# A transformer block with expert routing on one core: the last feed-forward layers rebuilt, and the opening's transfers put in another order

## The chip, the cores and the metric

The kernel runs on one core of a Trainium2 chip (trn2). The metric is the device time of one execution in microseconds (us). The five engines are TensorE (PE), VectorE (DVE), ScalarE (ACT), GpSimd (POOL) and SyncE (SP), which only issues transfers here. Each engine works through its own list of instructions in order, and engines wait for each other by semaphores. PSUM has eight banks of 128 partitions x 512 float32.

## The reference, cut to what matters

There are 8 batches of 256 tokens, width D = 256, 16 heads of 16.

```python
x = x + xattn0(layernorm(x), ctx, mask, W, b)      # "A" segments: masked softmax attention, then @ W.T + b
x = x + ffn0(layernorm(x), weight)                 # Hadamard, 4-bit quantised input, ternary weight
# third layer ("C" segments): attention with a bias per head, then a feed-forward layer
q, k, v = split(x_q @ Wq.T), split(x_kv @ Wk.T), split(x_kv @ Wv.T)
o = softmax(q @ k.T / 4 + bias) @ v
y = x_q + o @ Wo.T
h = gelu(layer_norm(y, g1, be1) @ W1.T + b1, approximate=False)     # 256 -> 1024
y = y + h @ W2.T + b2                                               # 1024 -> 256
x = x + layer_norm(y, g2, be2)
# fourth layer: each of 8 experts takes its 512 best tokens of all 2048
scores = softmax(layernorm(x) @ Wr); G, idx = top_k(scores.T, 512)
X_e = gelu(layernorm(x)[idx] @ W1[e] + b1[e]) @ W2[e] + b2[e]
out = x + scatter_add(G * X_e)
```

The routing (`top_k` over all 2048 tokens) cannot start before the last batch has gone through all three layers.

## The kernel before, in words

**Attention.** 16 segments run one after the other: A0, A1, A2, C0, A3, C1, ..., A7, C5, C6, C7, each of 16 units (2 query tiles x 8 pairs of heads). A loop counts slots `t`. In slot t, PE computes the scores of unit t+2 and transposes the probabilities of unit t (`ps_t`), and multiplies unit t-2 with the values (`ps_o`). DVE adds mask or bias and finds the row's extreme (`neg`, `neg_max`), ACT takes the exponential (`probs`) and the high half of the transposed probabilities (`p_hi`), DVE the low half (`p_lo`). Four units make a half: ACT copies it (`o_raw`), POOL adds its parts and normalises it (`attn`). Slot `ALL_UNITS` = 256 is the first without a new unit.

**What lies between the units.** `slots_of(b)` gives for each batch the slots at which the steps of its other layers stand on each engine: a table, not a planner. In a slot the units come first. The steps named below: `oc` (transposes of `attn`), `wo` (attention's output weights), `y` (sum and norm F), `z` (transposes of the normed rows), `f1` (first feed-forward weights, 8 pieces of two matmuls, into `ps_m[0]` and `ps_m[1]` in turn, copied to `hidT` with the bias by ACT two pieces at a time), `gelu` (Gelu in place on `hidT`), `f2` (second weights, into `ps_m[1]`), `y_ffn`, `ln_g`, `g_scale`, `x3` (sum, norm G with its two row vectors on POOL, sum into `x_all`), `ln_r`, `xr`, `logit` (norm R, its transposes and the routing logits).

**Stacks.** Before a segment, the two halves of k and q (`part_h` by ACT, `part_l`) go to `parts_dram` and come back in another layout: `k_stack` by four transfers into 32 partitions each, `q_stack` by eight into 16 partitions each. `q_stack` is zeroed once before (one memset of 128x4096 for each of two buffers). The stack of segment A1 lies where the ternary weight `w_b` is prepared (DVE `ve_start` in slots 0 to 2), so its loads wait for `wb_copied`.

**The opening.** SP's list stands in the code in its order: first inputs, mask and values of A0, `w_b`, row vectors, then the slots -16 to -1 (parts out, stacks in), then the weights.

## Time and profile before

| | us |
|---|---|
| median of 3 runs (983.73 to 984.74) | 983.77 |
| the profiled execution, own time | 983.23 |
| its span | 981.4 |
| busy PE / DVE / ACT / POOL | 769.3 / 660.2 / 616.5 / 430.6 |
| first scores of segment A0 | 29.46 |
| last unit's values copied | 654.28 |
| logits of the last batch end on PE | 712.07 |

Profile times count from the start of the span; the execution takes 1.83 us more than the span. No engine is busy throughout (PE 78%), and the shares are means over four very different stages: an opening in which almost only transfers run, attention, a tail after the last unit with the rest of batches 5, 6 and 7, and routing with the experts. So each stage is read by itself.

### The profile page before, as it was taken

Reading aid. Unit: us, or ns where it says so; the run is one execution under the profiler, and the core shown is the slowest. Engines: PE = TensorE matmul, PEld = TensorE weight load, DVE = VectorE, ACT = ScalarE, POOL = GpSimd, SP = SyncE. Lnnn points to the kernel's source line nnn. Section 1 sums busy time; section 2 is a strip of 40 time slices with the busy share of each in tenths; the row PEclk is TensorE's granted clock in tenths of the full one; section 3 lists DMA queues with packets and bytes.
Section 4 is the critical chain, followed back from the end, with each engine's and each line's share of the span. In section 5 each row is a group of like instructions: output and inputs, shape, how many; then the busy total and the mean of one; then the engine's idle time right before and its main releaser. Section 6 shows DMA issues by size and latency. Waiting matters only on the chain. (4 is left out here: it accounts for less than half of the span.)

```text
span 981.4 us, 19294 instructions
## 1 busy us (share of the span) xinstructions
PE 769.3 (78%) x6377; PEld 676.4 (69%) x6377; DVE 660.2 (67%) x2037; ACT 616.5 (63%) x1275; POOL 430.6 (44%) x626
## 2 busy tenths in 40 slices
PE   0566887887897987987989878878532799999995
PEld 0556776776786776876878768766421588888885
DVE  2686799786885986886787677542176366666651
ACT  1485777787787778679669758762010566666662
POOL 5154245264453554355244244143202456666654
PEclk9798789898998998999899998899655799999998
DMA  8598458668278477566645849200040234455532
GB/s 210 150 263 239 96 109 208 194 134 201 92 158 193 109 161 202 132 142 182 140 118 137 181 136 236 77 22 22 21 129 19 91 107 121 126 130 130 129 65 33
DMA packets 100290, 131.14 MB, mean 134 GB/s; under 512 B 8160, under 2 KB 72160, under 8 KB 100192
## 3 DMA queue, kind: packets, MB, share of 16 engines
q1 hardware_dynamic: 94048, 121.52, 48.8%
q0 software_dynamic: 6144, 8.39, 4.9%
q8 instruction: 52, 0.85, 0.4%
q14 instruction: 46, 0.38, 0.1%
HBM read 104.72 MB, written 25.17 MB: 132 GB/s over the span
## 5 line engine op out<-in xcount | busy, mean ns | idle before, releaser
L810 ACT ACTIVATE probs<-neg,neg_max 128x256 f32<-128x256 f32 x512 | 233.1, 507 | 108.5 <-DVE neg_max L659 105.4
L666 DVE TENSOR_TENSOR p_lo<-ps_t,p_hi 128x512 f16<-128x512 f32 x256 | 176.4, 689 | 108.5 <-ACT p_hi L817 108.4
L393 PE MATMUL ps_t<-ident,probs 128*128 128x128 f32 x1024 | 171.9, 294 | 59.8 <-ACT probs L810 59.3
L383 PE MATMUL ps_s<-k_stack,q_stack 128*128 128x256 f32 x512 | 147.2, 371 | 40.3 <-DMA q_stack<-parts_dram 21.3
L393 PEld LDWEIGHTS ps_t<-ident,probs 128*128 128x128 f32 x1024 | 124.3, 149 | 76.9 <-ACT probs L810 76.6
L817 ACT ACTIVATE p_hi<-ps_t 128x512 f16<-128x512 f32 x256 | 150.5, 588 | 27.5 <-PE ps_t L393 26.2
L383 PEld LDWEIGHTS ps_s<-k_stack,q_stack 128*128 128x128 f32 x512 | 94.6, 205 | 56.6 <-issue 30.8
L659 DVE CUSTOM_DVE_ANT_0 neg<-ps_s,bias_t 128x256 f32<-128x256 f32 x256 | 96.7, 415 | 13.8 <-PE ps_s L383 11.1
L1023 POOL TENSOR_TENSOR o_sum<-o_raw 128x128 f32<-128x128 f32 x64 | 30.2, 472 | 165.4 <-ACT o_raw L896 165.4
L659 DVE CUSTOM_DVE_ANT_0 neg<-ps_s,mask_add 128x256 f32<-128x256 f32 x224 | 84.1, 414 | 22.5 <-PE ps_s L383 22.3
L1329 DVE TENSOR_TENSOR hid_l<-hid_e,hid_h 128x512 fp32r<-128x512 f32 x64 | 69.4, 1115 | 40.2 <-ACT hid_e L1433 21.0
L413 PE MATMUL ps_o<-v_parts,p_hi 128*128 128x49 bf16 x1024 | 90.9, 189 | 0.9 <-DVE p_lo L666 0.9
L413 PE MATMUL ps_o<-v_parts,p_lo 128*128 128x49 bf16 x1024 | 89.4, 187 | 0.0
L1469 POOL DMA_INDIRECT out<-y_g,idx x32 | 52.8, 1649 | 67.7 <-ACT y_g L1447 59.5
L572 PE MATMUL ps_m<-w,hidT 128*128 128x256 f32 x256 | 76.0, 437 | 6.1 <-DVE part_l L673 5.3
L413 PEld LDWEIGHTS ps_o<-v_parts,p_hi 128*128 128x128 f16 x1024 | 79.2, 100 | 1.5 <-issue 1.3
L1399 PE MATMUL ps_o<-w_h,hid_h 128*128 128x256 f32 x256 | 75.3, 294 | 2.8 <-DVE hid_l L1329 2.7
L1399 PE MATMUL ps_o<-w_l,hid_h 128*128 128x256 f32 x256 | 72.3, 283 | 0.0
L1399 PE MATMUL ps_o<-w_h,hid_l 128*128 128x256 f32 x256 | 72.3, 282 | 0.0
L413 PEld LDWEIGHTS ps_o<-v_parts,p_lo 128*128 128x128 f16 x1024 | 68.1, 100 | 4.3
L555 PE MATMUL ps_m<-nrmT,w 128*128 128x256 f32 x256 | 68.8, 397 | 1.1 <-ACT nrmT L869 1.1
L1455 POOL DMA_INDIRECT xg<-normed_dram,idx x32 | 36.3, 1133 | 62.3 <-DVE idx L1302 45.7
(231 smaller groups left out, 1750.9 us busy)
## 6 DMA issues: line engine op xcount, KB each, us to landing
bias_t<-in_bias SPq DMA_DIRECT2D x64, 512.0 KB, 6.7
k_stack<-parts_dram SPq DMA_DIRECT2D x64, 256.0 KB, 4.3
q_stack<-parts_dram SPq DMA_DIRECT2D x128, 128.0 KB, 4.8
parts_dram<-part_h SPq DMA_DIRECT2D x32, 256.0 KB, 3.4
parts_dram<-part_l SPq DMA_DIRECT2D x32, 256.0 KB, 2.6
w1e<-in_w1e SPq DMA_DIRECT2D x8, 1024.0 KB
w2e<-in_w2e SPq DMA_DIRECT2D x8, 1024.0 KB, 5.7
ctxT_A<-in_ctxT SPq DMA_DIRECT2D x8, 256.0 KB, 5.7
```

The costliest lines, as they stand in the source:

```text
L383: ins = nc.tensor.matmul(ps_s[U % 2][:, i * SEQ:(i + 1) * SEQ], q_stack[g % 2][:, h % 2, j, c, qt * P:(qt + 1) * P], k_stack[g % 2][:, j, ...
L393: ins = nc.tensor.matmul(ps_t[U % 2][:, (i * QT + kb) * P:(i * QT + kb + 1) * P], probs[:, U % 2, i, kb * P:(kb + 1) * P], ident[:, :], st ...
L413: ins = nc.tensor.matmul(ps_o[half][:, col:col + VW], part[:, U % 4, (i * QT + kb) * P:(i * QT + kb + 1) * P], v_parts[g % 2][:, kb, h, :] ...
L555: ins = nc.tensor.matmul(ps_m[hc // 2 % 2][:, (hc % 2) * SEQ:(hc % 2 + 1) * SEQ], w_1[:, c, hc * P:(hc + 1) * P], nrmT[:, c, :], start=(c ...
L572: ins = nc.tensor.matmul(ps_m[1][:, tile * D:(tile + 1) * D], hidT[:, hc, tile * P:(tile + 1) * P], w_2[:, hc, :], start=(hc == 0), stop=( ...
L659: ins = nc.vector.tensor_tensor_reduce(neg[:, U % 4, i, :], ps_s[U % 2][:, i * SEQ:(i + 1) * SEQ], add, -1.0, 3.0e38, ALU.add, ALU.min, ne ...
L666: nc.vector.tensor_tensor(p_lo[:, U % 4, :], ps_t[U % 2][:, :], p_hi[:, U % 4, :], ALU.subtract).then_inc(lo_ready, 1)
L810: ins = nc.scalar.activation(probs[:, U % 2, i, :], neg[:, U % 4, i, :], ACT.Exp, bias=neg_max[:, U % 4, i:i + 1], scale=-1.0)
L817: nc.scalar.activation(p_hi[:, U % 4, :], ps_t[U % 2][:, :], ACT.Copy).then_inc(hi_ready, 1)
L1329: nc.vector.tensor_tensor(hid_l[:, hc, :], hid_e[:, hc % 4, :], hid_h[:, hc, :].bitcast(F32), ALU.subtract).then_inc(S["hid_ready"], 1)
L1399: ins = nc.tensor.matmul(ps_o[i][:, (st % 2) * D:(st % 2 + 1) * D], hid[:, hc, st * P:(st + 1) * P], w[:, hc, :], start=(n == 0), stop=(n ...
L1469: nc.gpsimd.indirect_dma_start(out, bass.IndirectOffsetOnAxis(ap=idx[e % 4][:, st:st + 1], axis=0), y_g[:, st, :], None, compute_op=ALU.ad ...
```

## The change

Three things.

**The last feed-forward layers.** In batch 6, `f1` stands earlier, two pieces to a slot in the last five slots of attention. In batch 7, `f1` writes to four banks that attention no longer uses (`ps_s[0]`, `ps_s[1]`, `ps_t[0]`, `ps_t[1]`), ACT takes Gelu with the bias straight from them into `hidT`, and `f2` goes quarter by quarter into `ps_o[0]` and `ps_o[1]`, each quarter as soon as its Gelu is there. Norm G of batch 7 is two DVE instructions for each tile, with one sum on POOL ahead of it. The slots of batch 7 and of `xr` and `logit` of batches 5 and 6 are set anew. ACT loads the Gelu table by an instruction on a scratch tile at slot 256.

**The opening.** `parts_out` and the stack loads of A0 stand directly behind the four first loads, everything else behind them. The zeroing of `q_stack[0]` moves from DVE to POOL, and A0's `part_l` of k from POOL to DVE. POOL and DVE no longer wait for the constants. `x_biased` of batch 0 stands behind the mask and values in POOL's list, and so the zeroing of `q_stack[1]` too.

**One scratch instruction** has ACT load its first table ahead of its first wait.

```diff
-LAST_SLOT = ALL_UNITS + 3 * UNITS
+LAST_SLOT = ALL_UNITS + 2 * UNITS
@@ slots_of
+        at.update(ln_a=early, ln_a_apply=early + 1, x_biased=early + 15, mask=early + 3, va=early + 4)
...
+    if b == 7:
+        at.update(oc=end + 2, wo=(end + 4, end + 4), y=end + 4, ln_f_apply=end + 5, yb=end + 6, z=end + 7,
...
@@ TensorE, batch 7
+        ps_last = [ps_s[0], ps_s[1], ps_t[0], ps_t[1]]
+        def pe_last_ffn(pe, t):
...
+                    for hc in (2 * n, 2 * n + 1):
+                        for c in range(DC):
+                            ins = nc.tensor.matmul(ps_last[n][:, (hc % 2) * SEQ:(hc % 2 + 1) * SEQ],
+                                                   w_1[:, c, hc * P:(hc + 1) * P], nrmT[:, c, :],
+                                                   start=(c == 0), stop=(c == DC - 1))
+                    ins.then_inc(S["f1_out"], 1)
+            for n in range(FC // 2):
+                if t == AT[b]["f2"][n]:
+                    pe.wait_ge(S["gelu_done"], b + n + 1)
...
+                        for tile in range(QT):
+                            ins = nc.tensor.matmul(ps_o[tile][:, 0:D], hidT[:, hc, tile * P:(tile + 1) * P],
+                                                   w_2[:, hc, :], start=(hc == 0), stop=(hc == FC - 1))
@@ ScalarE
+            for n in range(FC // 2 if b == NB - 1 else 0):
+                if t == at["f1"][2 * n]:
+                    ac.wait_ge(S["f1_out"], b * 4 + n + 1)
...
+                        ins = nc.scalar.activation(hidT[:, hc, :], ps_last[n][:, i * SEQ:(i + 1) * SEQ], ACT.Gelu,
+                                                   bias=cols[:, 2 * DC + hc:2 * DC + hc + 1])
+                if t == ALL_UNITS:
+                    nc.scalar.activation(warm[:, 1:2], warm[:, 0:1], ACT.Gelu)
@@ VectorE
+            if t == at["k_a"] and b == 0:
+                ve.wait_ge(S["part_h"], 1)
+                nc.vector.tensor_tensor(part_l[:, :, :], ctxT[A][:, :, :], part_h[:, :, :].bitcast(F32),
+                                        ALU.subtract).then_inc(S["part_l"], 1)
...
+            if t == at["g_scale"] and b == NB - 1:
...
+                    ins = nc.vector.scalar_tensor_tensor(nrm["G"][:, n, :], y_of(b)[:, n, :], mv["G"][:, n, 0:1],
+                                                         rows[:, 2, :], ALU.subtract, ALU.mult)
...
+                    ins = nc.vector.scalar_tensor_tensor(x_all[:, 2 * b + n, :], nrm["G"][:, n, :], rstd["G"][:, n:n + 1],
+                                                         x_all[:, 2 * b + n, :], ALU.mult, ALU.add)
...
             if s == 0:
+                ve.wait_ge(ld["const"], 16 * N_CONST)
+                nc.vector.tensor_copy(ident_b[:, :], ident[:, :])
@@ GpSimd
+            if t == at["ln_g"] - 1 and b == NB - 1:
+                nc.gpsimd.tensor_tensor(xpair(b), xpair(b), rows[:, 3:4, :].to_broadcast([P, QT, D]),
+                                        ALU.add).then_inc(S["g_added"], 1)
...
         def po_start(po):
+            nc.gpsimd.memset(q_stack[0][:, :, :, :, :].bitcast(F32), 0.0).then_inc(S["q_zero_0"], 1)
@@ SyncE
+            parts_out(A, 0, "k")
+            k_in(A, 0, (0, 1))
+            parts_out(A, 0, "q")
+            k_in(A, 0, (2, 3))
+            q_in(A, 0)
             load_mask(0)
             load_va(0)
+            load_a(1)
+            sp.dma_start(x_all[:, QT:2 * QT, :], a["x"][1]).then_inc(ld["x1"], 16)
             sp.dma_start(w_b[:, :, :], a["w_b"]).then_inc(ld["w_b"], 16)
...
-            for t in range(-UNITS, 0):
-                slot(t)
```

SP's list in the opening, before (`parts_dram` holds the halves on their way to the stacks):

```order
L1618 DMA ident<-in_ident 128x128
L1497 DMA mask_int<-in_mask 128x2x256
L1501 DMA v_raw_A<-in_ctx 128x2x256
L1621 DMA w_b<-in_w_b 128x2x256
L1623 DMA rows<-in_rows 128x256 x4
L1624 DMA x_all<-in_x 128x2x256
L1526 DMA parts_dram<-part_h 128x512
L1528 DMA parts_dram<-part_l 128x512
L1543 DMA k_stack<-parts_dram 32x4x512 x4
L1493 DMA ctxT_A<-in_ctxT 128x2x256
```

And now:

```order
L1696 DMA ident<-in_ident 128x128
L1604 DMA parts_dram<-part_h 128x512
L1606 DMA parts_dram<-part_l 128x512
L1621 DMA k_stack<-parts_dram 32x4x512
L1621 DMA k_stack<-parts_dram 32x4x512
L1604 DMA parts_dram<-part_h 128x512
L1606 DMA parts_dram<-part_l 128x512
L1621 DMA k_stack<-parts_dram 32x4x512
L1621 DMA k_stack<-parts_dram 32x4x512
```

Nothing stands between the constants and the parts any more, and mask, values, `w_b` and rows come after the eight loads of `q_stack`.

POOL's list behind the first norm, before:

```order
L953 TENSOR_TENSOR part_l<-ctxT_A,part_h 128x512
L958 TENSOR_TENSOR x_all<-x_all,rows 128x512
L963 TENSOR_SCALAR mask_add<-mask_int 128x512
L934 CAST v_parts<-v_raw_A 128x16x16 x2
L936 TENSOR_TENSOR v_rest<-v_raw_A,v_parts 128x256 x2
L938 CAST v_parts<-v_rest 128x16x16 x2
L940 TENSOR_TENSOR v_raw_A<-v_rest,v_parts 128x256 x2
L942 CAST v_parts<-v_raw_A 128x16x16 x2
L1110 MEMSET q_stack 128x4096
L953 TENSOR_TENSOR part_l<-ctxT_A,part_h 128x512
```

And now:

```order
L1039 TENSOR_SCALAR mask_add<-mask_int 128x512
L1010 CAST v_parts<-v_raw_A 128x16x16 x2
L1012 TENSOR_TENSOR v_rest<-v_raw_A,v_parts 128x256 x2
L1014 CAST v_parts<-v_rest 128x16x16 x2
L1016 TENSOR_TENSOR v_raw_A<-v_rest,v_parts 128x256 x2
L1018 CAST v_parts<-v_raw_A 128x16x16 x2
L1034 TENSOR_TENSOR x_all<-x_all,rows 128x512
L1188 MEMSET q_stack 128x4096
L1029 TENSOR_TENSOR part_l<-ctxT_A,part_h 128x512
```

The chain starts with the mask, whose load is now late in SP's list; the sum of rows and the second memset follow the values.

PE's list after the last unit, before (`nrm_R` are the transposes for routing, `attn` and `w_o` attention's output, L555 is `f1`, L572 `f2`):

```order
L555 MATMUL ps_m<-nrmT,w 128x256 x6
L327 MATMUL ps_m<-ident,nrm_R 128x128 x4
L589 MATMUL ps_m<-w_r,nrmT_c 128x8 x4
L327 MATMUL ps_m<-ident,attn 128x128 x4
L335 MATMUL ps_m<-w_o,nrmT 128x256 x2
L572 MATMUL ps_m<-w,hidT 128x256 x4
L335 MATMUL ps_m<-w_o,nrmT 128x256 x2
L572 MATMUL ps_m<-w,hidT 128x256 x12
L327 MATMUL ps_m<-ident,nrm_F 128x128 x4
L555 MATMUL ps_m<-nrmT,w 128x256 x16
L327 MATMUL ps_m<-ident,nrm_R 128x128 x4
L589 MATMUL ps_m<-w_r,nrmT_c 128x8 x4
```

And now (L580 is `f2` of batch 6, L618 and L629 are `f1` and `f2` of batch 7):

```order
L335 MATMUL ps_m<-ident,attn 128x128 x4
L580 MATMUL ps_m<-w,hidT 128x256 x2
L343 MATMUL ps_m<-w_o,nrmT 128x256 x4
L580 MATMUL ps_m<-w,hidT 128x256 x10
L335 MATMUL ps_m<-ident,nrm_F 128x128 x4
L580 MATMUL ps_m<-w,hidT 128x256 x4
L618 MATMUL ps_s<-nrmT,w 128x256 x8
L618 MATMUL ps_t<-nrmT,w 128x256 x4
L629 MATMUL ps_o<-w,hidT 128x256 x4
L618 MATMUL ps_t<-nrmT,w 128x256 x4
L629 MATMUL ps_o<-w,hidT 128x256 x12
L335 MATMUL ps_m<-ident,nrm_R 128x128 x4
```

Three of `f1`'s pieces of batch 6 are gone from here, the transposes and logits of batch 6 stand behind `f2` of batch 7 instead of between its two layers, and `f1` and `f2` of batch 7 interleave.

## Rows read from the trace of the kernel before

**Rows 1.** Busy time by stage, the tail: stretch, length, each engine, PE clock, DMA
```profile
654.28:712.07 57.79, 37.54 (x160) 30.66 (x159) 11.38 (x36) 15.25 (x25) 14.83 (x20) 0.81 0.06 22
```
**Rows 2.** Timeline of SP's issues, opening: start, length, line, what
```profile
6.61 0.47 SPq L1526 DMA_DIRECT2D parts_dram<-part_h  x1
...
11.36 1.75 SPq L1543 DMA_DIRECT2D k_stack<-parts_dram  x4
...
19.84 3.60 SPq L1555 DMA_DIRECT2D q_stack<-parts_dram  x8
23.48 0.43 SPq L1497 DMA_DIRECT2D mask_int<-in_mask  x1
```
**Rows 3.** Tile parts_dram, 0 to 47 us: issue to landing
```profile
DMA to landing us min/median/max: 2.0/4.6/6.3
```
**Rows 4.** Tile k_stack, the same
```profile
DMA to landing us min/median/max: 3.0/4.3/5.9
```
**Rows 5.** Tile q_stack, the same
```profile
DMA to landing us min/median/max: 2.9/4.7/6.3
```
**Rows 6.** Tile mask_int, the same
```profile
DMA to landing us min/median/max: 3.9/5.2/6.6
```
**Rows 7.** Timeline of DVE, opening and first units; idle before it in brackets
```profile
8.20 1.68 DVE L633 TENSOR_SCALAR nrm_A<-x_all,mv_A,rstd_A 128x256 f32<-128x256 f32 x2 [1.26 <-POOL rstd_A L923]
...
30.38 0.42 DVE L659 CUSTOM_DVE_ANT_0 neg<-ps_s,mask_add 128x256 f32<-128x256 f32 x1 [17.53 <-PE ps_s L383]
...
34.55 0.68 DVE L1068 TENSOR_REDUCE w_b_abs<-w_b 128x2 f32<-128x512 f32 x1
35.26 0.61 DVE L1069 TENSOR_SCALAR w_b_scale<-w_b_abs 128x2 f32<-128x2 f32 x1
...
36.31 0.42 DVE L659 CUSTOM_DVE_ANT_0 neg<-ps_s,mask_add 128x256 f32<-128x256 f32 x1
```
**Rows 8.** Timeline of POOL, the same
```profile
8.15 1.25 POOL L953 TENSOR_TENSOR part_l<-ctxT_A,part_h 128x512 fp32r<-128x512 f32 x1
...
11.39 1.95 POOL L963 TENSOR_SCALAR mask_add<-mask_int 128x512 f32<-128x512 int32 x1
13.40 0.76 POOL L934 CAST v_parts<-v_raw_A 128x256 bf16<-128x256 f32 x2
...
18.49 3.51 POOL L1110 MEMSET q_stack<- 128x4096 f32 x1
...
34.57 1.27 POOL L953 TENSOR_TENSOR part_l<-ctxT_A,part_h 128x512 fp32r<-128x512 f32 x1 [12.57 <-ACT part_h L822]
```
**Rows 9.** Timeline of PE, last unit and tail
```profile
649.92 0.66 PE L393 MATMUL ps_t<-ident,probs 128*128 128x128 f32 x4 [0.58 <-ACT probs L810]
...
662.98 2.07 PE L335 MATMUL ps_m<-w_o,nrmT 128*128 128x256 f32 x4 [2.24 <-ACT nrmT L865]
...
668.05 5.34 PE L572 MATMUL ps_m<-w,hidT 128*128 128x256 f32 x24
...
674.94 7.17 PE L555 MATMUL ps_m<-nrmT,w 128*128 128x256 f32 x32 [1.11 <-ACT nrmT L869]
...
687.54 10.04 PE L572 MATMUL ps_m<-w,hidT 128*128 128x256 f32 x32 [0.84 <-ACT hidT L885]
708.40 1.12 PE L327 MATMUL ps_m<-ident,nrm_R 128*128 128x128 f32 x4 [10.82 <-DVE nrm_R L633]
```
**Rows 10.** Timeline of ACT, tail
```profile
659.16 1.28 ACT L885 ACT_TABLE_LOAD   x1
660.45 2.00 ACT L885 ACTIVATE hidT<-hidT 128x1024 f32<-128x1024 f32 x2
```
**Rows 11.** Timeline of DVE, tail
```profile
668.32 0.69 DVE L748 TENSOR_TENSOR y_attn<-ps_m,xq_res 128x512 f32<-128x512 f32 x1 [7.86 <-PE ps_m L335]
...
697.69 0.69 DVE L756 TENSOR_TENSOR y_attn<-ps_m,y_attn 128x512 f32<-128x512 f32 x1 [10.78 <-PE ps_m L572]
...
705.38 0.75 DVE L618 BATCH_NORM_STATS2 st_R<-x_all 128x6 f32<-128x256 f32 x2 [4.05 <-POOL x_all L1014]
```

## What the change should do to the time, predicted before it ran

> **What bounds the kernel now.** The page says that no engine is busy throughout, so I read by stages and took two of them: those in which the change moves something. In the stretches view of the tail the reader is to see 57.8 us in which PE is busy 37.5 and DVE, ACT and POOL 11 to 15 [rows 1]: a chain in which one engine at a time works and the others wait. The timelines of the tail show its links: attention's output weights at 662.98, norm F at 668.32, `f1` of batch 7 at 674.94, `f2` at 687.54, norm G at 697.69, norm R at 705.38, its transposes at 708.40 [rows 9 to 11]. Everything behind 708.40 (logits, routing, experts) is unchanged and starts from it, so what the tail gives goes fully into the end.
>
> In the opening the chain is of transfers. SP's issues show the waits: `part_h` goes out at 6.61, but the first load of `k_stack`, which needs it, at 11.36; `q_stack`'s loads begin at 19.84 [rows 2] and the last lands at about 23.0 + 6.3 = 29.3 [rows 5]. DVE's first score pass is at 30.38 [rows 7]. Attention moves with that start: its loads for later segments hang on its own engines, so I carry a shift of the start to the end in full.
>
> **The opening, part by part.** Before, 1.5 MB of other loads lay ahead of `part_h` in SP's queue. Now only the first four do, and these have landed, since `part_h` waits for them. With the shortest landing, 2.0 [rows 3], the out-transfer issued at about 6.5 is there at 8.5, where it was 11.36. From there the queue is full and I add pieces. `k_stack`: first landing 11.4 + 3.0 = 14.4, last (issued 12.7) + 5.9 = 18.6 [rows 2, 4], so 1.4 us each. `q_stack`: 19.84 + 2.9 = 22.7 to 29.3 is 0.94 each [rows 2, 5]. Two further transfers of 256 KB lay between 18.6 and 19.84, so 0.6 each. New: first piece of k 11.5, second 12.9, the two parts of q 14.1 (they are ready: norm A at 8.20 no longer waits behind POOL's `part_l` [rows 7, 8]), two pieces of k 16.9, eight of q 24.5. The mask, before issued behind `q_stack` with a landing of 6.6, came at 23.48 + 6.6 = 30.1 [rows 2, 6], 0.75 behind the last q; now 25.25. That is a new wait: POOL needs 1.95 for it [rows 8], and the first pass cannot start before 27.3. Scores are ready earlier (25.7), so the mask is late next. Gain so far 30.38 - 27.4 = **3.0 us**. Its bounds: 1.5, if the landings after 8.5 keep the 3.0 of a queue's first piece at each wait, and 4.
>
> The price stands on DVE. Before, POOL had finished the values (13.40 to 18.49) and the zeroing of `q_stack[1]` (3.51) while DVE was idle [rows 8]. Now the values follow the mask (27.3 to 32.5), then the sum with rows (1.27, as the other additions of 128x512), then the memset (33.8 to 37.3), all beside DVE's burst for `w_b`, and DVE has little idle time there. The trace shows what POOL does to DVE's small instructions: `w_b_scale`, 128x2, took 0.61 and ended at 35.87, just as POOL's instruction of 34.57 + 1.27 did; and norm A's first pass from 8.20 to 9.88 spanned POOL's of 8.15 to 9.40 [rows 7, 8]. So some DVE instructions stand until POOL's is through. No row has a memset as POOL's part, so bounds: nothing (a memset does not block) and 3.5 (its whole length). By the nearest rows, in which the whole instruction was waited for, I take the whole. Working: DVE reaches the new cast of `ident_b` 4.2 behind its first pass (34.55 - 30.38), at 31.6; cast 0.5, reduction 0.7, `w_b_scale` behind the sum at 33.8, one `w_b_half`, then the memset has begun and the next waits until 37.3; POOL's own delay by DVE's cast adds about 0.3. The pass of unit 3, at 36.31 before [rows 7], comes at 37.9: **+1.6 us** net for the whole opening. Without the block by the memset it is at 34.3, -2.0.
>
> The Trainium skill, "SBUF — State Buffer", section "Who interferes with whom", says that DVE in its two-port modes and GpSimd take one shared port pair as a lock for the whole instruction. The two rows above agree; that a GpSimd memset holds it too, no row here shows. By that rule the opening costs as I forecast; by the memset's absence from the trace alone it could as well gain 2.0.
>
> Other edits of the opening are at nothing: the zeroing of `q_stack[0]` on POOL (3.5 us from about 1.7) is done at 5.2, ahead of the constants; the loads of `w_b` and rows land 3 to 6 us behind the mask, when DVE and POOL first want them, and if not, the wait falls on the same DVE stretch; ACT's first table load is hidden by the constants' load either way.
>
> **The tail, part by part.** (a) *End of attention to norm F of batch 7.* Before, the last probability transposes are at 649.92 [rows 9]. A pair of pieces of `f1` costs 8 records of 7.17/32 = 0.224, so 1.8 us; batch 6 has now four pairs in five slots instead of four single pieces. PE then transposes the last unit near 652.7 instead of 649.9, and `p_lo` of the last unit ends at 654.5. ACT: last bias copy to 654.7, table load 1.28 [rows 10], a copy for routing, then attention's copy at 656.8, where it was 654.28 [rows 1]. That is 2.5 late, and it is the table load that is late, in front of the copy. But then PE has nothing in its way: Gelu of batch 6 (2.00 [rows 10]) 657.3 to 659.3, `attn`'s transposes 659, their copy 660.1, one piece of `f2`, both halves of `wo` together. The first half of `wo` took 2.07 for 4 records, double of 0.224 each, after an idle time of 2.24 [rows 9]; I expect the same once. Norm F's sum starts at 664.3, before 668.32 [rows 11]: **-4.0**.
>
> (b) *To `f1` of batch 7.* Ten rows of `f2` (20 records x 5.34/24 = 4.45), transposes 0.6, eight more records 1.8 beside ACT's copy: 671.0. Before 674.94 - 668.32 = 6.6, now 6.7: **+0.1**.
>
> (c) *`f1` and `f2` of batch 7.* Before 674.94 to 697.69: 22.75, in it ACT's copies and Gelu (682 to 687.5) and `f2` in 10.04 where 32 records at the rate of `f2` of batch 6 take 7.1 [rows 9, 11]. Now PE never waits for all of Gelu: ACT's two instructions for a pair are below the pair's 1.8 on PE. 7.17 + 7.12 + 0.1 = 14.4: **-8.35**. Gelu from PSUM does not stand in the trace; bounds are 0.42 for one (the in-place 1.0 for 1024 columns scaled down, plus its start) and 1.0; only above 0.9 would ACT pace PE, at most +1.
>
> (d) *Norm G.* Before 697.69 to 705.38 = 7.7 [rows 11]. Now sum 0.85, statistics 1.1, the copy of batch 6's logits (PE does these behind `f2`: 2.6 us, so it is the logits that are late here, not POOL's root), two pairs of DVE instructions of 0.95: 4.6. **-3.1**. The 3.0 from 705.38 to 708.40 stay.
>
> Sum of the tail: -4.0 + 0.1 - 8.35 - 3.1 = -15.35. With the opening -15.35 + 1.6 = -13.8, from the profiled execution's 983.23 to 969.4. That execution lies 0.5 below the median of the runs shown, so the forecast is **970.0**.
>
> **Rivals.**
> *The memset does not block DVE.* For it: no row has one. Against: both rows in which POOL and a small DVE instruction meet. Then -15.35 - 2.0, so 966.4.
> *The tail gives less.* Attention's end loses more than it wins: pairs of `f1` delay scores, PE falls to 1.2 GHz more often in the short gaps between 656 and 660, and another 24 records run at double time. +5.4: about 975.4. For it: 2.07 in [rows 9]. Against: the granted clock of the tail was 0.81 with gaps of 5 to 11 us, which now shrink [rows 1].
> *Slower than before: PE stays at 1.2 GHz through the tail.* Its work from `wo` to the end of `f2` of batch 7 is 23.2 us at the full rate; all of it at double time is +23.2, so 970.0 + 23.2 = 993. The kernel becomes slower once more than 60% of that work (13.8 of 23.2) runs so. For it: `f2` at 687.54 ran at 0.31 per record, between both rates. Against: 674.94 to 682.1, after an idle time of 1.11, ran at 0.224 throughout, and the new tail has no longer gap before `f2` ends.
> *It does not do what it says in the opening.* If `q_stack`'s pieces wait for the parts of q longer than the queue is full, the first pass is no earlier than 29, and the opening costs 3.2: 971.6. I keep it inside the forecast's own range.
>
> **How the numbers follow.** Forecast 0.57, own range 967.5 to 973. No block by the memset 0.25, less in the tail 0.13, slow clock through the tail 0.03, something better than all of these 0.02. Range: down to 964, which takes in the second case with the bound of 4 us for the opening's gain, up to 975.5, which takes in most of the third. About 0.2% of the time, 2 us, is what a measurement can tell from no change. Faster 0.96, since only the slow clock in its worse half and an unforeseen wait reach 982; same 0.015; slower 0.025.
>
> **What would show it.** Opening: first load of `k_stack` at about 8.5; last of `q_stack` landed near 24.5; first pass at 27.4 with the idle time before it ended by POOL's mask; one DVE instruction of 128x2 or 128x256 with 2 to 3.5 us beside POOL's memset (right), or all below 0.7 (the second case); pass of unit 3 at 37.9. Tail, counted from the last probability transposes: attention's copy behind a table load; `f1` and `f2` of batch 7 together in 14 to 15 us with a granted clock near 1; from `y_ffn` to norm R 4.6 us. The forecast is wrong if `f2` shows waits for Gelu above 0.5 us each, if the stretch from the last unit's copy to norm R's transposes is over 44 us (before 54.1), or if the pass of unit 3 is outside 34 to 39.

## The result, and the profile after

The changed kernel takes 966.4 us (median of 4, 964.0 to 970.5) against 983.75 for the kernel before beside it: ratio 0.983, 95% interval 0.981 to 0.985. In a later comparison it took 963.1 (median of 6) against 984.7, ratio 0.979 (0.976 to 0.982). The forecast was 970.0 in 964.0 to 975.5.

The profiled execution is the longest of the first four: 970.47, span 968.6, against 983.23 and 981.4 before. Its 12.8 us split at two landmarks of the trace, each counted from the one before it. The first is ACT's copy of `o_raw` number 60 of 0 to 63 (half 60 below), which lies ahead of all that the change moves in the tail. The second is the first transpose of norm R's output of batch 7.

| stretch | before | after | difference | forecast |
|---|---|---|---|---|
| start to the pass of unit 3 | 36.31 | 36.95 | +0.64 | +1.6 |
| from there to the copy of half 60 | 585.26 | 589.23 | +3.97 | 0 |
| half 60 to norm R's transposes | 86.83 | 70.97 | -15.86 | -15.35 |
| from there to the end | 273.0 | 271.45 | -1.55 | 0 |

**The tail.** PE, after. A row is start, length, engine, line, operation, count, and in brackets the idle time before it and what ended it.

```profile
658.16 0.60 PE L401 MATMUL ps_t<-ident,probs 128*128 128x128 f32 x4
...
666.76 2.93 PE L343 MATMUL ps_m<-w_o,nrmT 128*128 128x256 f32 x8
669.53 4.48 PE L580 MATMUL ps_m<-w,hidT 128*128 128x256 f32 x20
...
676.01 3.62 PE L618 MATMUL ps_s<-nrmT,w 128*128 128x256 f32 x16
679.47 1.89 PE L618 MATMUL ps_t<-nrmT,w 128*128 128x256 f32 x8
681.19 1.89 PE L629 MATMUL ps_o<-w,hidT 128*128 128x256 f32 x8
682.92 1.89 PE L618 MATMUL ps_t<-nrmT,w 128*128 128x256 f32 x8
684.65 5.34 PE L629 MATMUL ps_o<-w,hidT 128*128 128x256 f32 x24
...
697.15 1.12 PE L335 MATMUL ps_m<-ident,nrm_R 128*128 128x128 f32 x4 [4.99 <-DVE nrm_R L674]
```

From 676.01 to 690 PE issues `f1` and `f2` of batch 7 with no gap; none of the five rows has a bracket. Before, the same 64 records stood with an idle stretch between them, and `f2` took 10.04 [rows 9]. The stretches of `f1` and `f2` in after: length, busy time of PE, PEld, DVE, ACT, POOL with counts, granted clock, DMA share, GB/s; then the whole tail, which answers to [rows 1]:

```profile
676.01:689.99 13.98, 13.98 (x67) 12.28 (x66) 4.69 (x13) 3.36 (x8) 6.89 (x8) 1.00 0.12 39
666.76:669.50 2.74, 2.74 (x9) 2.25 (x8) 0.00 (x0) 0.00 (x0) 0.00 (x0) 0.62 0.00 0
662.07:700.82 38.75, 32.21 (x144) 27.95 (x144) 12.85 (x39) 9.80 (x18) 12.24 (x18) 0.81 0.08 28
```

and in before the stretch in which `f2` of batch 7 ran:

```profile
687.54:697.60 10.06, 10.04 (x32) 8.04 (x32) 0.00 (x0) 0.00 (x0) 0.00 (x0) 0.71 0.00 0
```

The reader is to see the clock beside the length: 32 records of `f2` at a granted 0.71 take 10.04, and at 1.00 they take their 7.2 (1.89 + 5.34). The 8 records of `wo` ran at 0.62 and took 2.93; in another execution of the same code (`after_again` below) they took 1.95. ACT and DVE in the same tail, after:

```profile
660.20 1.28 ACT L975 ACT_TABLE_LOAD   x1
...
662.07 0.49 ACT L970 COPY o_raw<-ps_o 128x392 f32<-128x392 f32 x1
662.44 2.01 ACT L950 ACTIVATE hidT<-hidT 128x1024 f32<-128x1024 f32 x2
...
684.85 0.84 ACT L958 ACTIVATE hidT<-ps_t,cols 128x256 f32<-128x256 f32 x2 [2.61 <-PE ps_t L618]
```
```profile
669.80 0.69 DVE L793 TENSOR_TENSOR y_attn<-ps_m,xq_res 128x512 f32<-128x512 f32 x1 [5.49 <-PE ps_m L343]
...
690.10 0.75 DVE L806 TENSOR_TENSOR y_attn<-ps_o,y_attn 128x256 f32<-128x256 f32 x2 [2.27 <-PE ps_o L629]
...
692.29 0.89 DVE L817 SCALAR_TENSOR_TENSOR nrm_G<-y_attn,mv_G,rows 128x256 f32<-128x256 f32 x2
...
694.13 0.75 DVE L659 BATCH_NORM_STATS2 st_R<-x_all 128x6 f32<-128x256 f32 x2
```

A pair of Gelus from PSUM takes 0.84, under half of the pair's 1.8 on PE: ACT waits for PE here, not the reverse.

**The opening.** SP's issues, after:

```profile
5.98 0.33 SPq L1604 DMA_DIRECT2D parts_dram<-part_h  x1
...
8.03 0.80 SPq L1621 DMA_DIRECT2D k_stack<-parts_dram  x2
...
12.86 3.58 SPq L1633 DMA_DIRECT2D q_stack<-parts_dram  x8
16.49 0.43 SPq L1575 DMA_DIRECT2D mask_int<-in_mask  x1
```

`k_stack`'s first load goes out 3.3 us earlier than in [rows 2], `q_stack`'s 7.0 earlier. DVE and then POOL, after:

```profile
25.80 0.42 DVE L700 CUSTOM_DVE_ANT_0 neg<-ps_s,mask_add 128x256 f32<-128x256 f32 x1 [15.80 <-POOL mask_add L1039]
...
31.09 4.60 DVE L1147 TENSOR_SCALAR w_b_half<-w_b_scale 128x2 f32<-128x2 f32 x1
...
35.72 1.19 DVE L1148 TENSOR_SCALAR w_b_half<-w_b_scale 128x2 f32<-128x2 f32 x1
...
36.95 0.42 DVE L700 CUSTOM_DVE_ANT_0 neg<-ps_s,mask_add 128x256 f32<-128x256 f32 x1
```
```profile
23.81 1.95 POOL L1039 TENSOR_SCALAR mask_add<-mask_int 128x512 f32<-128x512 int32 x1 [17.86 <-DMA mask_int<-in_mask]
...
30.95 1.27 POOL L1034 TENSOR_TENSOR x_all<-x_all,rows 128x512 f32<-128x512 f32 x1
32.16 3.51 POOL L1188 MEMSET q_stack<- 128x4096 f32 x1
35.63 1.26 POOL L1029 TENSOR_TENSOR part_l<-ctxT_A,part_h 128x512 fp32r<-128x512 f32 x1
```

The first pass waits for the mask, as the bracket says, and begins 4.6 us earlier than in [rows 7]. Eleven us later all of that is gone: an instruction on 128x2 elements ends at 35.69, with POOL's memset at 35.67, and the next at 36.91, with POOL's subtraction at 36.89.

### The profile page after: what moved, and what is told of

It is laid out like the page before. It is cut to its first block and busy times, and to the rows that moved or that the text cites. A ratio compares the mean times of both kernels' runs of the same rounds, so it can differ in the third digit from the quotient of the medians.

```text
span 968.6 us, 19298 instructions
## 1 busy us (share of the span) xinstructions
PE 771.3 (80%) x6377; PEld 681.5 (70%) x6377; DVE 664.4 (69%) x2041; ACT 613.4 (63%) x1275; POOL 429.9 (44%) x624
## 5 line engine op out<-in xcount | busy, mean ns | idle before, releaser
L391 PE MATMUL ps_s<-k_stack,q_stack 128*128 128x256 f32 x512 | 150.0, 377 | 44.1 <-DVE neg_max L700 18.2
L700 DVE CUSTOM_DVE_ANT_0 neg<-ps_s,mask_add 128x256 f32<-128x256 f32 x224 | 83.9, 412 | 20.7 <-POOL mask_add L1039 15.8
L580 PE MATMUL ps_m<-w,hidT 128*128 128x256 f32 x224 | 68.1, 440 | 6.7 <-DVE part_l L714 6.7
L563 PE MATMUL ps_m<-nrmT,w 128*128 128x256 f32 x224 | 63.1, 408 | 0.2 <-ACT nrmT L934 0.2
```

What stands on the lines that cost most here:

```text
L391: ins = nc.tensor.matmul(ps_s[U % 2][:, i * SEQ:(i + 1) * SEQ], q_stack[g % 2][:, h % 2, j, c, qt * P:(qt + 1) * P], k_stack[g % 2][:, j, ...
L563: ins = nc.tensor.matmul(ps_m[hc // 2 % 2][:, (hc % 2) * SEQ:(hc % 2 + 1) * SEQ], w_1[:, c, hc * P:(hc + 1) * P], nrmT[:, c, :], start=(c ...
L580: ins = nc.tensor.matmul(ps_m[1][:, tile * D:(tile + 1) * D], hidT[:, hc, tile * P:(tile + 1) * P], w_2[:, hc, :], start=(hc == 0), stop=( ...
L700: ins = nc.vector.tensor_tensor_reduce(neg[:, U % 4, i, :], ps_s[U % 2][:, i * SEQ:(i + 1) * SEQ], add, -1.0, 3.0e38, ALU.add, ALU.min, ne ...
```

## The experiments

### The two halves apart, and the zeroing moved

`tail_only` is the kernel before with the changes of the tail alone, `open_only` with those of the opening alone:

```diff
 # tail_only
-LAST_SLOT = ALL_UNITS + 3 * UNITS
+LAST_SLOT = ALL_UNITS + 2 * UNITS
 ...
+        ps_last = [ps_s[0], ps_s[1], ps_t[0], ps_t[1]]
 # open_only
+            parts_out(A, 0, "k")
+            k_in(A, 0, (0, 1))
+            parts_out(A, 0, "q")
+            k_in(A, 0, (2, 3))
+            q_in(A, 0)
```

> The kernel before with only the rebuilt last feed-forward layers (slots of batches 5 to 7, four banks, Gelu from PSUM, f2 by quarters, norm G in two instructions, early Gelu table). Theory: the tail gives nearly everything and the opening nothing, because what its transfers gain is lost to POOL's block of DVE. Then this kernel is at 966 to 969 (ratio 0.982 to 0.985) and the stretch from the last unit's probability transposes to the transposes of norm R of batch 7 is 39 us (58.5 before). Rival: the opening contributed; then this kernel is at 970 or more.

> The kernel before with only the opening's new order. Theory: first score pass at 25.8 (30.4 before), but unit 3's pass at 37.0 (36.3 before), since one w_b_half of 128x2 stands 4.6 us beside POOL's sum and memset and the next 1.2 beside part_l; total 983.5 to 985, the same as before within noise. Rival: the opening helps although the trace of one execution does not show it, 979 to 981.

`early_zero` is the changed kernel with POOL's zeroing of `q_stack[1]` ahead of the mask's work:

```diff
-                if t == 0:
+                if t == -UNITS + 1:
                     po_zero_stack(po)
```

> The changed kernel with one edit: POOL zeroes q_stack[1] directly behind the first norm's root (about 6 us), when it has nothing to do, not at the first unit. Theory (POOL's memset holds DVE's two-port instructions for its whole length): w_b_half takes at most 1.3 beside the sum with rows, unit 3's pass comes at 32.5 to 33.5 instead of 37.0, and the kernel is 3.5 to 4.5 us faster than the changed one, 962 to 963. Rival (the 4.6 us of w_b_half have another cause, a late load or a semaphore): w_b_half stays at 4 or more and the time at 966.

`before_late_zero` does the opposite, in the kernel before: it holds the zeroing back until DVE is in its burst.

```diff
                 if t == 0:
+                    po.wait_ge(lo_ready, 1)
                     po_zero_stack(po)
```

> The kernel before with one edit: POOL's zeroing of q_stack[1] waits for the first low part (34.6) instead of running at 18.5. The loads stay as they are. Theory: w_b_scale at 35.3 stands until POOL's memset is over at 38.1, a following one until part_l is over at 39.4; unit 3's pass moves from 36.3 to 39.5 and the total by +3, to 987. Rival (DVE is not blocked by a memset): w_b_scale stays below 0.7 and the total at 984.

Measured, in one comparison (before: 983.94, median of 23; the trace's columns are from one execution each):

| kernel | time | ratio (95%) | first pass | pass of unit 3 | between |
|---|---|---|---|---|---|
| before | 983.94 | | 30.38 | 36.31 | 5.93 |
| `tail_only` | 963.11 | 0.980 (0.977 to 0.982) | 28.98 | 34.90 | 5.92 |
| `open_only` | 979.82 | 0.997 (0.995 to 0.999) | 22.49 | 33.64 | 11.15 |
| `early_zero` | 963.82 | 0.981 (0.978 to 0.984) | 28.26 | 35.96 | 7.70 |
| `before_late_zero` | 986.79 | 1.004 (1.001 to 1.006) | 30.55 | 39.86 | 9.31 |

The block is shown in both directions. POOL, then DVE, of `before_late_zero`:

```profile
34.86 3.51 POOL L1111 MEMSET q_stack<- 128x4096 f32 x1 [16.26 <-DVE p_lo L666]
38.34 1.26 POOL L953 TENSOR_TENSOR part_l<-ctxT_A,part_h 128x512 fp32r<-128x512 f32 x1
```
```profile
35.43 2.96 DVE L1070 TENSOR_SCALAR w_b_scale<-w_b_abs 128x2 f32<-128x2 f32 x1
...
38.43 1.19 DVE L1071 TENSOR_SCALAR w_b_half<-w_b_scale 128x2 f32<-128x2 f32 x1
...
39.86 0.42 DVE L659 CUSTOM_DVE_ANT_0 neg<-ps_s,mask_add 128x256 f32<-128x256 f32 x1
```

`w_b_scale` starts 0.57 behind the memset and ends at 38.39, 0.02 behind the memset's end. In [rows 7] the same instruction took 0.61. With the memset early, in `early_zero`, the 4.60 is gone from this place:

```profile
33.55 1.15 DVE L1147 TENSOR_SCALAR w_b_half<-w_b_scale 128x2 f32<-128x2 f32 x1
34.74 1.18 DVE L1148 TENSOR_SCALAR w_b_half<-w_b_scale 128x2 f32<-128x2 f32 x1
```

But the block has only moved. The early memset runs while DVE applies norm A, whose rows must leave as the parts of q. POOL and DVE of `early_zero`:

```profile
5.76 3.50 POOL L1188 MEMSET q_stack<- 128x4096 f32 x1
```
```profile
6.25 3.48 DVE L674 TENSOR_SCALAR nrm_A<-x_all,mv_A,rstd_A 128x256 f32<-128x256 f32 x2
```

and DVE of the changed kernel at the same place:

```profile
6.60 0.73 DVE L674 TENSOR_SCALAR nrm_A<-x_all,mv_A,rstd_A 128x256 f32<-128x256 f32 x2
```

SP issues the high part of q at 11.61 instead of 9.22, the first load of `q_stack` at 13.86 instead of 12.86 and the mask at 17.54 instead of 16.49, and the first pass comes at 28.26. In `open_early_zero` below it is the same (3.65, 11.58, 13.83, 17.50, first pass 28.51).

That a memset on POOL holds DVE is settled: late, it costs 3.4 us of trace (9.31 against 5.93; 11.15 against 7.70). The kernel before, which is the same in all but this wait, becomes 2.9 us longer by it (interval 1.4 to 5.7), as its theory said. `early_zero` met its theory in `w_b_half` (1.15, at most 1.3) and missed it in the pass of unit 3: 35.96 and not 32.5 to 33.5.

For the whole change the tail is the gain: alone it brings 20.8 us, more than its theory gave it, and its trace took 38.4 from the last probability transposes to norm R's (39 in the theory). The opening alone brings 4.1 (interval 1 to 5), which is its rival's time and not its theory's. The two don't add up: the whole change, at 0.983 and 0.979 in its two comparisons, is not faster than the tail alone at 0.980.

### The same kernel again, batch 6 at its old places, the opening with both, and the mask first

`after_again` has no edit. `old_slots_6` puts batch 6's `f1`, Gelu and `f2` and the logits of batches 5 and 6 back to where the kernel before has them, and batch 7 behind it:

```diff
     if b == 6:
-        at.update(f1=tuple(end - n for n in (5, 5, 4, 4, 3, 3, 2, 2)), f1_copy=(end - 4, end - 3, end - 2, end - 1),
-                  gelu=end + 1, f2=tuple(end + n for n in (3, 5, 5, 6, 6, 6, 8, 8)), y_ffn=end + 9, ln_g=end + 9,
 ...
+        at.update(gelu=end + 4, f2=tuple(end + n for n in (7, 7, 8, 8, 9, 9, 10, 10)), y_ffn=end + 10, ln_g=end + 10,
```

`open_early_zero` is `open_only` with the zeroing early. `mask_first` is `early_zero` with the mask and the values in SP's queue ahead of the last pieces of `k_stack`:

```diff
             parts_out(A, 0, "q")
-            k_in(A, 0, (2, 3))
-            q_in(A, 0)
             load_mask(0)
             load_va(0)
+            k_in(A, 0, (2, 3))
+            q_in(A, 0)
```

> The changed kernel once more, unchanged, to have its time and a second trace on the same chip as the next three. Theory: the time is 964 to 967; from the first score pass to unit 3's pass it is 11.15 us again, since POOL's instructions set it, while the first pass itself moves by a few us with the speed of the transfers (22.5 to 28.3 in three traces of this order so far); the second loss of attention (at the copies of 206 and 619 us) does not come back, since it was waits for bias loads and the clock of one execution. Rival: these losses belong to the change; then they stand at the same places.

> The changed kernel with batch 6's f1, Gelu and f2, and batch 7's attention output, at the slots of the kernel before; four banks, Gelu from PSUM, the quarters of f2 and the new norm G stay. Theory: this undoes the term from the end of attention to norm F (-3.1 to -4.9 in three traces), so from the copy of the half that ends near 620 us to norm F's sum of batch 7 it is 46 to 47 us instead of 42 to 43.6, and the total is 3 to 5 above the changed kernel. Rival: pairs of f1 in attention's last slots cost what they give later; then both are within 1 us.

> The kernel before with the opening's new order and POOL's zeroing of q_stack[1] at about 6 us instead of at the first unit; the tail is the old one. Theory: first pass as in the other kernels with this order, from it to unit 3's pass 7.7 us instead of 11.15, total 3.5 below the opening alone: 976 to 977. Rival (the opening alone gains by another way than its first pass): no difference to the opening alone, 979.8.

> The changed kernel with the early zeroing, the loads of A0's mask and values ahead of the second half of k_stack's loads instead of behind q_stack's, and the sum with rows of batch 0 at slot 4 instead of slot -1. Theory: POOL has done mask and values before the scores are there; the first pass follows the last load of q_stack by 1 to 1.3 us (2.5 in the changed kernel) though that load lands 1.3 later; from the first pass to unit 3's it is 6.2 to 7.3 us; 1 us below the kernel with the early zeroing alone, 4 to 5.5 below the changed one: 961 to 962. Rival: the two loads delay q_stack by more than they save, and it is no better than early zeroing alone.

Measured, in one comparison (before: 984.69, median of 17):

| kernel | time | ratio (95%) | pass of unit 3 | half 60 against before | half 60 to norm R's transposes |
|---|---|---|---|---|---|
| `after_again` | 963.14 | 0.979 (0.976 to 0.982) | 37.99 | -1.67 | 68.07 |
| `old_slots_6` | 969.81 | 0.985 (0.982 to 0.988) | 37.03 | +3.08 | 73.19 |
| `open_early_zero` | 981.12 | 0.996 (0.994 to 0.998) | 36.22 | -2.58 | 87.83 |
| `mask_first` | 961.28 | 0.978 (0.975 to 0.981) | 33.00 | -4.52 | 68.04 |

The same code reached half 60 at +4.61 in one execution and at -1.67 in the next. The +3.97 of the first table is so no cost of the change: from the pass of unit 3 to half 60 it took 589.2 in the first profile, 581.9 in this one and 585.3 before, and 581.0 to 587.6 in the other kernels. The -1.55 behind the tail is scatter too: that stretch, whose code nothing here changes, took 271.4 to 273.0 over all fourteen profiles. The largest step of the +3.97, 3.2 us, lies between halves 58 and 59, where DVE waited once for a transfer of the bias and the granted clock fell. From the view of waits (who for whom, us in total, times, longest) and that of stretches, after:

```profile
DVE neg L700 <- DMA bias_t<-in_bias: 3.0, 1, 3.0
```
```profile
607.40:618.90 11.50, 9.13 (x75) 8.15 (x73) 5.51 (x20) 7.41 (x19) 3.31 (x7) 0.85 0.96 263
```

and the same 75 records of PE in before, 3.2 us shorter:

```profile
606.00:614.30 8.30, 7.54 (x75) 6.85 (x73) 5.43 (x20) 7.35 (x19) 3.33 (x7) 1.00 1.07 334
```

`old_slots_6` shows that moving batch 6's `f1` into the last units of attention, with what follows it, is worth 0.6% (0.985 against 0.979; the intervals just clear each other), and the tail of its trace is 5.1 longer than that of `after_again`. Which of the moved steps brings how much, it doesn't tell. Its PE runs `wo` in two halves with pieces of batch 6's `f2` between them:

```profile
664.46 1.24 PE L342 MATMUL ps_m<-w_o,nrmT 128*128 128x256 f32 x4 [0.83 <-ACT nrmT L929]
665.49 3.51 PE L579 MATMUL ps_m<-w,hidT 128*128 128x256 f32 x8
668.84 1.03 PE L342 MATMUL ps_m<-w_o,nrmT 128*128 128x256 f32 x4
```

`open_early_zero` met its rival (981.1, where the theory had 976 to 977): its first pass came at 28.51, and what it gains behind that (7.71) it has at least in part lost ahead of it, as shown above.

`mask_first` has its memset ahead too, and norm A takes 3.61 beside it, but neither the mask nor a memset stands between its first pass and unit 3's, which it reaches at 33.00. It has the lowest median of all kernels, 961.28, clearly below the kernel before; against the changed kernel the intervals overlap (0.975 to 0.981 and 0.976 to 0.982), so I can't call it faster. Its DVE, where the pass now waits for PE's scores and no longer for the mask:

```profile
27.02 0.42 DVE L700 CUSTOM_DVE_ANT_0 neg<-ps_s,mask_add 128x256 f32<-128x256 f32 x1 [14.65 <-PE ps_s L391]
...
32.60 0.17 DVE L1147 TENSOR_SCALAR w_b_half<-w_b_scale 128x2 f32<-128x2 f32 x1
32.80 0.17 DVE L1148 TENSOR_SCALAR w_b_half<-w_b_scale 128x2 f32<-128x2 f32 x1
```

The instruction that stood for 4.60 takes 0.17 when POOL has nothing. In the changed kernel DVE and POOL are both idle from 10.0 to 23.8 us; the memset was not tried there.

### The tail's parts undone one by one

All four are the changed kernel. `gelu_wait_all` lets `f2` of batch 7 wait for all Gelus and not for its pair's; `gelu_in_place` has in addition bias copies first and Gelu in place in two large instructions, as before the change:

```diff
 # both
-                  f2=tuple(end + n for n in (11, 12, 13, 14)), ...
+                  f2=tuple(end + n for n in (13, 14, 14, 15)), ...
 # gelu_wait_all
-                    pe.wait_ge(S["gelu_done"], b + n + 1)
+                    pe.wait_ge(S["gelu_done"], b + FC // 2)
 # gelu_in_place
-                        ins = nc.scalar.activation(hidT[:, hc, :], ps_last[n][...], ACT.Gelu,
+                        ins = nc.scalar.activation(hidT[:, hc, :], ps_last[n][...], ACT.Identity,
 ...
+                                ins = nc.scalar.activation(hidden, hidden, ACT.Gelu)
```

`old_norm_g` gives norm G of batch 7 back its old form, with the multiplication and two additions on POOL; `no_warm_gelu` takes out the small Gelu that brings the table load forward:

```diff
 # old_norm_g
-            if t == at["g_scale"] and b < NB - 1:
+            if t == at["g_scale"]:
 ...
-            if t == at["x3"] and b < NB - 1:
+            if t == at["x3"]:
 # no_warm_gelu
-                if t == ALL_UNITS:
-                    nc.scalar.activation(warm[:, 1:2], warm[:, 0:1], ACT.Gelu)
```

> The changed kernel; f2 of batch 7 starts only when all four pairs have had their Gelu. Gelu still comes straight from PSUM. Theory: only the last pair's Gelu (0.84) is exposed, so from f1's start to y_ffn it is 15.0 to 15.3 us instead of 14.09 and the total is 1 above. Rival (the interleaving is what counts): 3 us or more, PE's clock falls in the gap.

> The changed kernel; batch 7 uses the four banks, but ACT copies with the bias and then takes Gelu in place in two instructions, as before, and f2 waits for both. Theory: the last pair's copy 0.84 and Gelu 2.0 are exposed, 17.1 to 17.4 us from f1's start to y_ffn if f2 keeps its rate, up to 20 if the gap of 3 us halves PE's clock for part of it; total 3 to 6 above the changed kernel. Of the 8.66 the change gained here that leaves 3 to 5.5 to the banks and the moved transposes and logits. Rival: the banks alone give it, under 15 us.

> The changed kernel with norm G of batch 7 in its old form: DVE applies it, POOL multiplies, adds and sums. Theory: from y_ffn to the statistics of norm R it is 8.5 us again instead of 4.8, total 3.7 above. Rival (the logits of batch 6, which DVE copies in between, set it anyway): below 1.

> The changed kernel without the instruction that loads the Gelu table at slot 256; the load comes with batch 6's Gelu, behind attention's last copy. Theory: attention's copy is 1.5 earlier, Gelu 0.3 to 0.9 later, and PE waits for Gelu then instead of for attn: from the last probability transposes to norm F's sum of batch 7 within 0.7 of the changed kernel's 11.6, total within 1. Rival (the load in front of the copy costs its 1.28): 1.3 better.

Measured, in one comparison (before: 982.89, median of 11). The trace's columns split the tail: half 60 to norm F's sum; from there to `f1`; `f1` and `f2`; from the feed-forward sum to the end of norm R's statistics:

| kernel | time | ratio (95%) | to norm F | to `f1` | `f1`, `f2` | norm G | all |
|---|---|---|---|---|---|---|---|
| before | 982.89 | | 46.75 | 6.62 | 22.75 | 8.48 | 86.83 |
| after (first profile) | | | 43.62 | 6.21 | 14.09 | 4.81 | 70.97 |
| `after_again` | | | 40.71 | 6.21 | 14.08 | 4.83 | 68.07 |
| `gelu_wait_all` | 966.49 | 0.985 (0.982 to 0.988) | 40.77 | 6.21 | 15.28 | 4.82 | 69.31 |
| `gelu_in_place` | 968.62 | 0.986 (0.983 to 0.989) | 40.97 | 6.22 | 17.31 | 4.82 | 71.56 |
| `old_norm_g` | 968.46 | 0.985 (0.983 to 0.989) | 43.67 | 6.21 | 14.09 | 8.53 | 74.73 |
| `no_warm_gelu` | 964.72 | 0.982 (0.979 to 0.984) | 42.91 | 6.21 | 14.08 | 4.82 | 70.25 |

In the rows of the changed kernel and its variants the three columns in the middle repeat to 0.02 us wherever their code is unchanged; the first scatters by 3 us, and the last with it. The old tail does not repeat so well: its `f1`, `f2` took 22.75, 23.86, 21.29 and 23.84 in `before`, `open_only`, `before_late_zero` and `open_early_zero`. The changed kernel itself was not timed in this comparison. So the parts of the tail are read from the trace, and the times (2 to 8 us between the lowest and the highest of each kernel) only agree in direction. PE of `gelu_in_place`:

```profile
673.50 3.62 PE L618 MATMUL ps_t<-nrmT,w 128*128 128x256 f32 x16
...
680.08 7.17 PE L629 MATMUL ps_o<-w,hidT 128*128 128x256 f32 x32 [2.96 <-ACT hidT L965]
```

The wait for pairs is worth 1.2 (15.28 - 14.08), Gelu from PSUM a further 2.0 (17.31 - 15.28). The other 5.4 (22.75 - 17.31) are neither. 2.9 of them are the rate of `f2` (10.04 against 7.17), and 2.5 the stretch between `f1` and `f2`: 2.96 here, 5.4 before (682.1 to 687.54 in [rows 9]), with PE's transposes and logits of batch 6 and ACT's copies in it. Over the four profiles with the old tail these are 4.0 to 6.6 in all, 1.4 to 2.9 by the rate (`f2` took 8.58 to 10.10) and 2.5 to 3.5 by the stretch. `f2` ran here at the full rate although PE had idled 2.96 just before; what in the old order brought the clock down, to 0.71 in the first profile, was not taken apart.

`old_norm_g` shows norm G's 3.7 alone: 8.53 against 4.82, and DVE's wait for POOL's addition, 4.05, is back as in [rows 11].

`no_warm_gelu` answered to neither expectation. Counted from the last probability transposes, norm F's sum comes at 12.68, against 10.67, 10.69 and 10.66 in `after_again`, `gelu_wait_all` and `mask_first`, and 11.64 in the first profile. PE shows why: a wait for Gelu, then `wo` at a lower rate.

```profile
658.64 2.08 PE L580 MATMUL ps_m<-w,hidT 128*128 128x256 f32 x4 [0.72 <-ACT hidT L950]
660.51 3.52 PE L343 MATMUL ps_m<-w_o,nrmT 128*128 128x256 f32 x8
```

Of the 2.0 against `after_again`, 1.6 is the rate of `wo` (3.52 against 1.95 for 8 records) and only 0.3 the later start of the piece of `f2` ahead of it. In the eight profiles whose code is the same up to there, `wo` took 1.95 to 2.94, so the one execution with 3.52 doesn't show that the table load's place is worth more than 0.3; its time, 964.72, doesn't show it either.

## Why the prediction was right, step by step

It was right in direction and in which part gains most. The time came 3.6 us below 970.0 in the first comparison, within the range, and 6.9 below in the second, 0.9 under the range's lower end of 964.0. In the tail the mechanism was right and its gain was put too small; the cost of the opening, +1.6, shows in the traces in part and in no time. The traces give each term:

- **(a) End of attention to norm F, forecast -4.0.** -3.1 in the first profile, -4.8, -4.4, -6.1 and -6.0 in `tail_only`, `early_zero`, `mask_first` and `after_again`. Of the two parts that I worked out, the last probability transposes came 3.6 later against half 60 in the first profile and 1.7 in `after_again` (forecast 2.8), and from these to norm F's sum it took 11.6 and 10.7 (forecast 11.6, before 18.4). The table load at 660.20 stands ahead of ACT's copy as forecast. The double time for `wo` that I carried from [rows 9] is the difference in the second part: 2.93 for its 8 records in the first profile, 1.95 in `after_again`. Four of the five gained more than my term.
- **(b) To `f1`, forecast +0.1.** -0.4. The ten rows of `f2` took 4.48 as worked out (4.45), but began 0.27 ahead of the sum; transposes and eight records behind them took 2.16, where I had 2.4.
- **(c) `f1` and `f2`, forecast -8.35.** -8.66: 14.09 against 14.4, in all profiles with this code within 0.01. Right, with the clock at 1.00; the side of the kernel before is one draw from 21.3 to 23.9.
- **(d) Norm G, forecast -3.1.** -3.67. The logits of batch 6 were not late: DVE waited 0.28 for them and copied in 0.17, where I had 0.75.
- **The opening, forecast +1.6.** +0.64 in the first profile; +0.15 as the mean of the eight profiles with the new order and the late memset (33.6 to 38.0) against 36.31. The old opening without an edit has one more profile, `tail_only`, with 34.90. Two steps missed in opposite directions. The first pass came at 25.80 and not 27.4, as the mask, issued at 16.49, was there at 23.8 where I had 25.25; over the eight it lay between 22.5 and 26.8. And the stretch from it to unit 3's pass was 0.65 longer than my 10.5: I let one `w_b_half` slip in between POOL's sum and its memset. It did not. The row of 4.60 spans the rest of the sum (to 32.2) and the memset (to 35.67), so the second `w_b_half` stood another 1.19 beside `part_l`, a third block that my sum did not have.

That DVE's instruction ends with POOL's agrees with the rule of the Trainium skill, "SBUF — State Buffer", section "Who interferes with whom", that the shared port pair is a lock held for the whole instruction. That a memset, which reads nothing, holds it too is what these runs add, and that a waiting instruction of DVE did not get in between the sum and the memset; it did between the memset and `part_l` (4.60, then 1.19), and in `early_zero` between the sum and `part_l` (1.15, then 1.18).

The rival in which the memset does not block (966.4) named the time that was measured, but for a wrong reason: the block is there. The tail gave 0.5 more than its sum in the first profile and 2.8 more as a mean of five (69.2, where four profiles with the old tail have 87.3). The rival with less in the tail and the one with a slow PE are out: the granted clock of `f1` and `f2` was 1.00. That the opening does not do what it says is out too, by SP's row at 12.86 and the first pass at 25.80, where that rival had 29.

**What stays open.** The sign of the opening. In the traces its eight profiles are on the average no earlier at the pass of unit 3 than the kernel before; in the times it saves 4.1 us alone and nothing that can be told on top of the tail (963.1 for the tail alone, 966.4 and 963.1 for the whole). What gives it its gain alone is not settled, and an attention that reaches half 60 up to 5.7 us earlier or 4.6 later than before, from one execution to the next, covers it in single profiles.

The early zeroing shows nothing in the times (0.996 against 0.997 for the opening alone, 0.981 against 0.979 and 0.983 for the whole), and the traces show at least a part of the reason: some of the 3.45 us that it gains behind the first pass (11.15 against 7.70) is paid ahead of it. With it the mask goes out at 17.5, against 15.8 to 16.5 in the eight profiles without, since norm A stood beside the memset. That is 1.0 to 1.8 us. It lands 8.7 and 9.0 later, against 4.7 to 8.7, and how much of that is the speed of the transfers alone isn't shown. Unit 3's pass comes at 35.96 and 36.22, against 36.46 as the mean of the eight.

## What to carry to other kernels

Read a change of the opening and one of the tail apart: a stretch from one landmark to another repeats to hundredths where engines alone set it, while one that hangs on transfers or on the granted clock scatters by microseconds, and one profile says nothing about it. Put POOL's long instructions, memsets too, where DVE is idle, and look at DVE's list there, not only at POOL's: a small instruction of DVE beside them can cost their whole rest, and two of POOL's in a row can be one wait. In a chain in which one engine at a time works, cut the hand-overs (a pair's result from PSUM rather than all of it in place): besides the waits that this took away here, `f2` ran at the full rate.

## What the runs showed of the hardware that was not expected

- A POOL memset of 128x4096 f32 (3.51 us) held DVE's 128x2 `w_b` scalings to its end in every run in which they met: 4.60 with the sum ahead of it, 2.96 from 0.57 behind its start. Norm A's two instructions of 128x256 took 3.48 to 3.65 beside it and 0.73 alone. Beside POOL's 128x512 instructions of 1.26 the same form took 1.15 to 1.19, and with POOL idle 0.17.
- PE kept the rate of 0.224 per record over 32 records after an idle time of 2.96 (`gelu_in_place`), and took 0.44 for each of the 8 records of `wo` in `no_warm_gelu`, where the gap shown just before is 0.72. With unchanged code the same 8 records took 1.95 to 2.94. The last gap alone does not tell what rate follows.
- The same opening gave a first pass between 22.5 and 26.8 us in eight executions; its mask landed 4.7 to 8.7 us behind its issue. That scatter is as large as what the reordering moves (30.38 to 25.80 in the first pair of profiles).
